# Two steps of a hand-written order moved later: a diagonal turn in a kernel-feature attention, query blocks in a retention layer

## The reference

```python
x = x + _L0_attn_ref(_layernorm(x), ...)    # Performer attention: 16 heads of 64, 64 features
x = x + _L0_xattn_ref(_layernorm(x), ctx, ...)  # causal and cross attention
x = x + _L0_ffn_ref(_layernorm(x), ...)     # mixture of 8 experts, top 2, with capacity
x = x + _L1_attn_ref(_layernorm(x), ...)    # retention: 16 heads of 16, decay gamma
x = x + _L1_xattn_ref(_layernorm(x), ctx, ...)  # two full attention blocks with GELU
x = x + _L1_ffn_ref(_layernorm(x), ...)     # 4 SwiGLU experts, top 1
```

```python
dd = einsum('bhnd,md->bhnm', dn * data, P)
diag = (sum(data * data, -1) * 0.5 * dn * dn)[..., None]
mx = max(dd, -1) if is_query else max(dd)
return ratio * (exp(dd - diag - mx) + EPS)
```

```python
q, k, v = split(x @ W_qkv.T);  k = _layernorm(k)
S = gamma * S + v_t[:, None] * k_t[None, :];  y_t = S q_t
```

## Time and profile before

| | us |
|---|---|
| median of 3 runs | 1647.88 |
| lowest and highest | 1645.28, 1648.71 |
| the profiled execution's own time | 1645.28 |
| its span in the profile | 1643.6 |

### The profile page before, as it was taken

One profiled execution on the slowest core, in us unless ns is written; L12 is line 12 of the kernel. 1 busy time (PEld: TensorE's weight loads), 2 busy tenths in 40 slices (PEclk: granted clock), 3 DMA queues, 4 the chain that ended last, 5 costly groups with the idle time before them and its releaser, 6 DMA issues.

```text
span 1643.6 us, 24086 instructions
## 1 busy us (share of the span) xinstructions
PE 1499.3 (91%) x9671; PEld 810.3 (49%) x9671; DVE 864.1 (53%) x1805; ACT 712.0 (43%) x1035; POOL 566.8 (34%) x643
## 2 busy tenths in 40 slices
PE   7999979999999987795899899998899999994997
PEld 4678853333333263583553333563233333574997
DVE  3255548888888454203673666325677774212221
ACT  4544223366666634331334445442355556422331
POOL 3043233623222122103021455511367778604111
PEclk9999989999999988897999999998699999995999
DMA  6000020000000018662300000223000000372100
GB/s 204 1 1 1 1 49 7 1 1 1 1 1 1 1 54 289 209 224 57 42 16 6 1 1 16 55 98 116 6 1 1 1 1 27 106 299 89 43 9 12
DMA packets 70339, 84.23 MB, mean 51 GB/s; under 512 B 24945, under 2 KB 55889, under 8 KB 69202
## 3 DMA queue, kind: packets, MB, share of 16 engines
q1 hardware_dynamic: 67395, 75.31, 14.5%
q0 software_dynamic: 2832, 7.38, 1.4%
HBM read 63.56 MB, written 19.51 MB: 51 GB/s over the span
## 4 chain that ended last, share of the span: by engine, by line
PE 83%; DVE 7%; DMA 3%; ACT 2%; POOL 2%; issue 2%; SPq 0%; POOLq 0%; DVEq 0%; ACTq 0%
PE psum L1366 14%; PE psum L1385 9%; PE psum L1331 6%; PE psum L3394 5%; PE psum L2683 4%; PE psum L693 3%; PE psum L2674 3%; PE psum L1407 3%; PE psum L1521 3%; DVE a_nm L1458 2%; PE psum L3405 2%; PE psum L2212 2%; PE psum L361 2%; PE psum L733 2%; PE psum L2652 2%; PE psum L681 2%
## 5 line engine op out<-in xcount | busy, mean ns | idle before, releaser
L1458 DVE TENSOR_REDUCE a_nm<-psum 128x1 f32<-128x512 f32 x384 | 250.6, 685 | 138.6 <-PE psum L1331 97.1
L1458 DVE TENSOR_REDUCE xa_nm<-psum 128x1 f32<-128x512 f32 x256 | 161.8, 681 | 14.8 <-PE psum L1331 11.6
L1420 ACT ACTIVATE xnT<-psum 128x1024 f32<-128x1024 f32 (+1 forms) x104 | 95.2, 960 | 58.8 <-PE psum L1366 52.9
L1420 ACT ACTIVATE a_w<-psum 128x1024 f32<-128x1024 f32 x86 | 83.8, 1021 | 71.6 <-PE psum L1366 57.3
L1366 PE MATMUL psum<-xa_cq,ctxT 32*128 32x512 f32 x512 | 113.4, 635 | 0.8 <-ACT xn L1420 0.8
L1331 PE MATMUL psum<-a2kr,a2qr 32*128 32x512 bf16 x256 | 87.2, 411 | 14.9 <-DVE a_nm L1458 14.2
L1366 PE MATMUL psum<-a2qT,a2kT 32*128 32x512 f32 x512 | 100.6, 624 | 0.0
L1331 PEld LDWEIGHTS psum<-a2kr,a2qr 32*128 32x128 bf16 x256 | 21.0, 92 | 125.7 <-DVE a_nm L1458 109.9
L1420 ACT ACTIVATE xn<-psum 128x1024 f32<-128x1024 f32 (+1 forms) x64 | 59.5, 971 | 49.9 <-PE psum L1366 49.8
L1331 PE MATMUL psum<-xa_ckr,xa_cqr 32*128 32x512 bf16 x256 | 69.3, 385 | 9.8 <-POOL xa_ckr L1567 5.1
L1362 PE MATMUL psum<-a_mrow,onesb 3*128 3x512 bf16 x384 | 70.4, 399 | 1.5 <-DVE a_mrow L1480 1.1
(11 more groups left out here) (542 smaller groups left out, 3372.1 us busy)
## 6 DMA issues: line engine op xcount, KB each, us to landing
mo_w<-in_L_ffn_W SPq DMA_DIRECT2D x14, 1024.0 KB, 7.0
sw_wv<-in_L_ffn_w_v SPq DMA_DIRECT2D x4, 2048.0 KB, 18.7
scratch_a2v<-co_stages SPq DMA_DIRECT2D x16, 256.0 KB, 2.5
scratch_a2k<-co_stages SPq DMA_DIRECT2D x16, 256.0 KB, 3.4
a2kT<-scratch_a2k SPq DMA_DIRECT2D x8, 512.0 KB, 7.9
a2v<-scratch_a2v SPq DMA_DIRECT2D x4, 1024.0 KB, 11.8
sw_wp<-in_L_ffn_w_proj SPq DMA_DIRECT2D x4, 1024.0 KB, 19.5
a1li<-in_L_xattn_a_li_w SPq DMA_DIRECT2D x2, 1024.0 KB, 6.3
```

Of the source, the lines that this page charges most:

```text
L1420: e.activation(self.weights(n, c)[:, 2 * jj:2 * jj + 2, lo:S], ps[:, pr:pr + 2, lo:S], ACT.Exp, scale=self.scale).then_inc(*self.weighed.m ...
L1458: e.tensor_reduce(self.nm[n % 3][:, q, part, h:h + 1], view, AX.X, ALU.max, negate=True).then_inc(*self.max_taken.mark(*i))
```

## The change

The diagonal of query pair 0 is turned behind the features and the diagonal of pair 1, as a step of the order, and no longer inside the projection of pair 2. In retention the two query blocks of batch 1 come behind the key turns and the second key norm; keys and values 4 to 7 now follow each other.

```diff
@@ -566,6 +566,8 @@
                 if pair + 2 < PAIRS:
                     yield "project", ("q", pair + 2)
                 yield "queries", pair + 1
+                if pair == 0:
+                    yield "turn_diagonal", ("q", 0)
             yield "contexts", pair
             if pair + 1 < PAIRS:
                 yield "turn_diagonal", ("q", pair + 1)
@@ -692,8 +694,6 @@
             for f in range(FC):
                 t = e.matmul(k.ps[:, bank, :], wt[:, f, chunk(pair)], k.xnT[:, f, cols(n)], start=f == 0, stop=f == FC - 1)
             t.then_inc(*self.projected.mark(which, pair, n))
-            if (which, pair, n) == ("q", 2, 0):
-                self.tensor_diagonal_turn(e, w, "q", 0)
 
     def features_free(self, which, pair, n):
         return (self.key_kept if which == "k" else self.query_scaled).at(pair, n)
@@ -2873,11 +2873,10 @@
 
         yield "key_norm", 0
         yield from (("queries", (m, 0)) for m in range(FC))
-        yield from (("keys_values", c) for c in range(SC, SC + 2))
-        yield from (("queries", (m, 1)) for m in range(FC))
-        yield from (("keys_values", c) for c in range(SC + 2, NC))
+        yield from (("keys_values", c) for c in range(SC, NC))
         yield from (("key_turn", (m, 0)) for m in range(FC))
         yield "key_norm", 1
+        yield from (("queries", (m, 1)) for m in range(FC))
         for c in range(NC + 2):
             if c < NC:
                 yield "scores", c
```

## The result

| | us |
|---|---|
| before: median of 20 runs (lowest, highest) | 1648.59 (1634.99, 1652.11) |
| after: median of 20 runs (lowest, highest) | 1657.80 (1646.93, 1660.94) |
| ratio of after to before, 95% interval | 1.0056 [1.0042, 1.0072] |
| the profiled execution of after, its span | 1649.24, 1647.5 |

In these 20 executions of each kernel the change makes it slower by 0.56%. The direction and the places were predicted; the median is 4.0 us above the forecast and 1.0 us above the range's end.

The account below looks back on a forecast made before the run. It took the DVE and ACT chain behind the diagonal to bound the Performer stretch, and squares, key norm, decay and state to bound retention's start. 1647.9 + 4.17 + 1.2 + 0.5 gave 1653.8 us, range 1650.0 to 1656.8.

Parts of the forecast that it names:

- Part one, the wait: Performer, 80 to 96 us: the later query turn delays the DVE and ACT chain and pair 1's turn by 4.17 us.
- Part one, the clock: Performer, behind the new pause: one half-clock stretch of 3.4 us costs 1.2 us, with ends 0 and 3.4.
- The choice of the pauses: Clock cost judged from pauses called nearest in size to 4.2 us: 5.14, and 1.29 with 2.33, each with 3.4 us at half.
- Part two: Retention, 790 to 814 us: moving batch 1's queries makes the decay 0.5 us later, with ends -0.9 and +2.2.
- The bank wait: Retention: scores 0 waits for DVE's last product of the moved queries, putting decay at 805.90 and not 805.43.
- The local sum: Performer wait, clock loss and retention together: 4.17 + 1.2 + 0.5 = 5.9 us.
- the rival of a recovered clock: At 1160 to 1192 us the shift lets the clock recover, returning up to 13.6 us, rather half; chance 0.07.
- the base: Whole kernel: the median of three executions before the change, 1647.88 us, to which 5.9 us was added.
- Pause without clock: Performer: the clock stays at 1.00 through the new pause, so 4.7 us in all, 1652.6 us; chance 0.17.
- Hidden: After the Performer: other PE work or a later wait absorbs the 4.2 us, time 1648 to 1650; chance 0.13.

Follow-up runs that it names:

- turn_fed9: Kernel before with only the later turn of query diagonal 0, plus 9 idle matmuls behind contexts 0 in the new pause; 1654.35 us, ratio 1.0037.
- after_again: The changed kernel run again without edits, 12 executions; 1655.01 us, ratio 1.0025.
- after_third: The changed kernel run a third time without edits; 1656.29 us, ratio 1.0037.
- queries_banks: Kernel before with only retention's batch 1 queries moved, but kept in their old banks; 1648.64 us, ratio 1.0000.
- queries_only: Kernel before with only retention's batch 1 queries moved as in the change; 1650.24 us, ratio 1.0013.
- turn_only: Kernel before with only the diagonal turn of query pair 0 moved as in the change; 1654.12 us, ratio 1.0019.
- turn_early: Kernel before with the turn of query diagonal 0 issued 0.86 us earlier, behind the first product of pair 2's first half; 1648.00 us, ratio 0.9992.
- pair_plain: Kernel before with the edits of turn_early and queries_banks together, no idle matmuls; 1648.84 us, ratio 0.9996.
- best: Kernel before with the edits of turn_early and queries_banks, plus idle matmuls (6, 6, 32 single) in the second attention block; 1661.38 us, ratio 1.0069.
- late_fed32: Kernel before with only idle matmuls (6, 6, then 32 single) in the second attention block's row-maximum pass; 1658.83 us, ratio 1.0062.

## Why the prediction was wrong in size and right in kind

- **Part one, the wait (4.17 us): right.** Turn at 87.43 (87.42), contexts 0 at 89.07 (88.94), turn of pair 1 at 95.30 (95.23) with 4.18 us of idle time. With the clock held up it measured 4.2 to 4.4 us (turn_fed9), and it was still there 450 us later.
- **Part one, the clock (1.2 us): near.** 1.4 us in three profiled executions, 2.2 in two; the term was set between no loss and one stretch lying wholly on dense work, and each of the five traces with the bare pause shows a loss. The choice of the pauses was not quite the nearest in size: before also has one of 3.11 us at 616 us, inside a longer stretch at half clock, and one of 2.50 us, and this was followed by 6.8 us at half. Rows 10 don't have it; 6.8 us is also what after_again and after_third showed. The pause and the window behind it:

```profile
225.01 2.13 PE L361 MATMUL psum<-ident,xn 128*128 128x128 f32 x8 [2.50 <-DVE xn L297]
...
225.00:232.00 7.00, 6.21 (x13) 3.23 (x14) 0.97 (x2) 1.56 (x4) 3.31 (x10) 0.51 0.36 90
```

- **Part two (0.5 us): right mechanism at its place.** The bank wait decides (queries_banks). Scores 0 came 1.1 us late as worked out; the decay 0.6 late in queries_only and 1.0 in after, where the clock fell within scores 0, which took 1.66 us in place of 1.17. The prediction took this as carried to the end. It wasn't: -0.4 to 0.7 us are left at 875 us, by where the half clock falls.
- **The local sum.** 4.2 + 1.4 to 2.2 + (-0.4 to 0.7) = 5.2 to 7.1 us, against 5.9. What the two edits do at their places was forecast well.
- **The step that failed: the sum has no term for the clock of the stages behind the two places, and its range comes from three executions.** The prediction carries 5.9 us to the end and adds nothing for the late half-clock stretches; their only place in it is the rival of a recovered clock, a gain with a chance of 0.07. The traces show between 550 and 1600 us +4.0 us in after_again and +6.8 in turn_only, -4.6 in after and -4.5 in after_third. On the way the lateness of each goes up by 7 to 9 us by 925 us and then down by 3 to 12. The range took the executions of the kernel before as spread from 1645.28 to 1648.71. Over all groups 156 of them run from 1635.0 to 1658.1 us (mean 1648.3, median 1649.1), and 44 of the change from 1639.7 to 1661.8 (mean 1655.0, median 1657.5). Of the 44, 29 stand at 1654 to 1662, 12 at 1646 to 1652 and 3 at 1640 to 1641. So the medians differ by 8.4 us (9.2 in the 20 executions of the result, 5.8 and 7.3 in the repeats, so how far the result lay above the forecast is in part the draw) and the means by 6.7. The difference of the means has a 95% interval of 4.7 to 8.5 us (by resampling the executions): it agrees with the 5.9 and with the local sum, and proves neither. In part the miss is also the base: 1647.88 from three executions, 1648.59 from 20. after_again and turn_only, at 1659 and 1660 us, are late by 10 and 12 us at 1600 us, of which 6.3 and 5.6 are from the Performer.
- **The rivals.** "Pause without clock" didn't happen. "Hidden" didn't either: the lateness is flat from 100 to 550 us. The recovered clock at 1160 us, given a chance of 0.07, was in two of the three traces of the change, as a property of an execution: it gave back 11.4 us in after and in after_third (11.7 to 0.3, 12.8 to 1.4) and nothing in after_again. It also came without any shift from the Performer, in queries_only (-1.3 to -12.6). That is why a profiled execution of after at 1649.24 us looks like no change at all.
- **Left open.** Why the median rose by more than the local sum: whether a shift of 6 us as such makes long late stretches more frequent. turn_early, which starts 0.9 us earlier (mean 1647.4), and queries_only (mean 1649.4) came with a wider spread: standard deviations of 7.0 and 6.6 us over 12 executions each, against 6.0 over the 44 of the change and 3.9 over the 156 of the kernel before. But queries_banks and pair_plain, which are shifted too, have 1.9 and 2.3. The shares of the groups may depend on the program; no run here shows by what rule.

## What to carry to other kernels

When a step is moved, look up what stands behind its consumer in the hand-written order: here DVE and ACT had a chain that hung on two transposes, and a turn issued 4.2 us later on PE made everything behind it 4.2 us late, up to 550 us at least, and the clock made it 5.6 to 6.4. A lateness at one instruction need not be a loss: the 1.0 us of the first decay in retention was 0.2 at the second. Undoing the rotation of buffers by hand (here three banks) tells whether a reorder loses through its order or through the buffers that it happens to get. Read an edit of a few microseconds from instructions matched between two traces, close to the edit; judge the whole by many executions and their groups, since one median, or one profile, can be 10 us away by the clock alone.

## What was unexpected in the hardware

- A half-clock stretch of 51.2 us with PE busy for 50.42 of 52 us (best), and of 44.4 us in late_fed32: being busy with a mix of 128-row and 32-row matmuls did not end it. late_fed32 with 12 fewer idle matmuls had 13.7 us in two executions, and best with 12 fewer 27.3 in one.
- Executions of one program came in groups 10 us apart (1640, 1650 and 1660 for after_again). The kernel before has its own: 9 of 156 executions stand at 1635 to 1637, and nearly all others at 1644 to 1654.
- The clock fell at 812.6 us, half a microsecond after the pause of 2.39 us ahead of scores 0 in after, and no other pause of PE lies between 798.4 us and this one. In before, a pause of 2.50 us that ended at 225.0 was followed by 6.8 us at half clock, and after the 1.37 us at 91 us it stayed up.
- The same pause of 4.18 us was followed by 3.4 us at half clock in three traces and had the clock down for 6.8 us, from 2.0 or 1.8 us ahead of its end, in two.
